# Routing of a two-layer transformer's second attention moved from a stage of its own into the attention's steps

## The reference

```python
def _L1_attn_ref(x, Wkqv, bkqv, Wp, bp):             # 16 heads, keys and queries of 128, values of 8
    ...
    A = jnp.einsum('bhnd,bhmd->bhnm', q, k) / jnp.sqrt(jnp.float32(Dm))
    A = jax.nn.softmax(jnp.where(mask[None, None], A, -jnp.inf), axis=-1)    # causal
    sa = jnp.einsum('bhnm,bhmd->bnhd', A, v).reshape(Bm, Nm, Dm)
    return sa @ Wp + bp

x = _layernorm(x + _L1_attn_ref(x, ...))             # called x3 below

def _moe_forward(x, centroid, Wg, bg, W1, b1, W2, b2):       # 8 experts, 2 per token
    d2 = sum(xs * xs) + sum(centroid * centroid) - 2.0 * (xs @ centroid.T)
    dist = jnp.sqrt(jnp.maximum(d2, 1e-12))
    w, sel = jax.lax.top_k(dist, K)                  # the two farthest centroids
    w = softmax(w)
    out = sum over the chosen e of w_e * ((silu(xs @ Wg[e] + bg[e]) * (xs @ W1[e] + b1[e])) @ W2[e] + b2[e])
```

## Time and profile before

| | us |
|---|---|
| median of three runs (2514.0, 2520.67, 2524.66) | 2520.67 |
| the profiled execution's own time | 2512.72 |
| its span | 2511.0 |
| `layer0`, 0 to 599.5 | 599.5 |
| `attention1`, 599.5 to 1863.1 | 1263.6 |
| `route1`, 1863.1 to 2126.8 | 263.7 |
| `experts1`, 2126.8 to 2433 | 306.2 |
| `combine1`, 2433 to 2511 | 78 |

### The profile page before, as it was taken

One profiled execution on the slowest core, in us unless ns is written; L12 is line 12 of the kernel. 1 busy time (PEld: TensorE's weight loads), 2 busy tenths in 40 slices (PEclk: granted clock), 3 DMA queues, 4 the chain that ended last, 5 costly groups with the idle time before them and its releaser, 6 DMA issues. The chain is left out here.

```text
span 2511.0 us, 67688 instructions
## 1 busy us (share of the span) xinstructions
PE 2272.6 (91%) x16828; PEld 1709.2 (68%) x16829; DVE 1888.3 (75%) x6162; ACT 1605.6 (64%) x4162; POOL 1015.9 (40%) x1979
## 2 busy tenths in 40 slices
PE   5999999997999999999999999999989991999960
PEld 3777777774666666666666666666657771999960
DVE  6888888871888888888888888888864552666658
ACT  2555555553777777777777777777753331667664
POOL 5676676671222222222222222222213666555542
PEclk9999999997999999999999999999985555999985
DMA  1011001001000000000000000000021111222225
GB/s 33 28 31 33 30 29 33 27 26 47 1 0 0 0 0 0 0 0 0 0 0 0 0 0 0 0 0 0 0 70 61 58 62 52 57 60 60 61 69 168
DMA packets 77583, 68.83 MB, mean 27 GB/s; under 512 B 10573, under 2 KB 70490, under 8 KB 77036
## 3 DMA queue, kind: packets, MB, share of 16 engines
q1 hardware_dynamic: 68830, 50.88, 6.9%
q0 software_dynamic: 8704, 17.39, 2.1%
HBM read 33.55 MB, written 22.62 MB: 22 GB/s over the span
## 5 line engine op out<-in xcount | busy, mean ns | idle before, releaser
L1017 DVE SCALAR_TENSOR_TENSOR restT<-ps_t,leadT 128x512 f16<-128x512 f32 (+1 forms) x768 | 462.8, 603 | 147.3 <-ACT leadT L978 95.3
L892 PE MATMUL ps_s<-xT_all,qm 128*128 (+1 forms) x1024 | 492.8, 563 | 11.8 <-issue 10.9
L978 ACT ACTIVATE leadT<-ps_t 128x512 f16<-128x512 f32 (+1 forms) x768 | 400.4, 522 | 151.0 <-PE ps_t L908 151.0
L908 PEld LDWEIGHTS ps_t<-ident,p 128*128 128x128 f32 x2560 | 320.8, 141 | 216.4 <-issue 180.9
L908 PE MATMUL ps_t<-ident,p 128*128 128x128 f32 x2560 | 405.4, 273 | 1.2 <-DVE restT L1017 0.5
L846 POOL CAST v_parts<-v_all 128x36 bf16 (+1 forms) x256 | 56.3, 220 | 805.8 <-PE ps_o L921 805.8
L1008 DVE CUSTOM_DVE_ANT_0 ps_s<-ps_s,mask 128x512 f32<-128x512 f32 (+1 forms) x512 | 320.1, 625 | 46.7 <-PE ps_s L892 46.6
L970 ACT ACTIVATE p<-ps_s,neg_max 128x512 f32<-128x512 f32 (+1 forms) x512 | 323.5, 632 | 4.6 <-DVE neg_max L1008 4.1
L892 PEld LDWEIGHTS ps_low<-xT_all,qm 128*128 128x128 f32 x1024 | 195.1, 191 | 135.8 <-issue 122.5
L884 PE MATMUL ps_qm<-xT_all,m_head 128*128 (+1 forms) x512 | 275.2, 619 | 0.3 <-issue 0.3
L267 POOL TENSOR_TENSOR pv_prod<-probs,kv 128x2048 f32<-128x2048 f32 x64 | 259.6, 4080 | 0.1
(11 more groups left out here) (222 smaller groups left out, 4570.2 us busy)
## 6 DMA issues: line engine op xcount, KB each, us to landing
row_in<-rows_dram SPq DMA_DIRECT2D x136, 64.5 KB, 1.9
y<-results SPq DMA_DIRECT2D x32, 256.0 KB, 3.3
xT<-in_xT SPq DMA_DIRECT2D x32, 128.0 KB, 2.2
xres<-in_xT SPq DMA_DIRECT2D x32, 128.0 KB, 2.1
x_all<-x SPq DMA_DIRECT2D x32, 128.0 KB, 2.0
xT_all<-x2T SPq DMA_DIRECT2D x32, 128.0 KB, 2.0
x_all<-x SPq DMA_DIRECT2D x16, 256.0 KB, 2.3
out_x<-x SPq DMA_DIRECT2D x16, 256.0 KB, 2.2
```

Of the source, the lines that this page charges most:

```text
L892: mm = pe.matmul(ps_s[n], qm[j][:, n * P:(n + 1) * P], xT_all[:, bass.ds(sequence(u) * S, (n + 1) * P)], start=True, stop=True)
L908: mm = pe.transpose(ps_t[g][:, at + n * P:at + (n + 1) * P], probs[i][:, n * P:(n + 1) * P], ident[:, :])
L978: act.activation(leadT[j][g][:, :], ps_t[g][:, 0:width[g]], ACT.Copy, scale=RAISE)\
L1017: dve.scalar_tensor_tensor(out=restT[j][g][:, :], in0=ps_t[g][:, 0:width[g]], scalar=RAISE, in1=leadT[j][g][:, :], op0=ALU.mult, op1=ALU.s ...
```

## The change

`route1` is gone. A sequence's routing is done within the attention's steps of the next sequence: in step h of sequence b, each engine calls `route(b - 1, h)` behind its `step`. Only the last sequence's routing comes after the attention. One PSUM bank (`ps_r`, P × 512) that was spare serves it in turn for the transposes, for two halves of products, and for the count.

```diff
+                for b in range(2):
+                    for h in range(H):
+                        one(b, h)
+                        if b:
+                            route(b - 1, h)
+                with eng.Fori(2, NG - 1) as b:
+                    for h in range(H):
+                        step(b, h, True, True, True, True)
+                        route(b - 1, h)
+                for h in range(H):
+                    one(NG - 1, h)
+                    route(NG - 2, h)
```

```diff
+                def bias_x2T(g):
+                    pool.wait_ge(c_ready, 5)
+                    when(pool, proj_ps, 2 * g)
+                    pool.tensor_tensor(x2T[:, :], xT_all[:, bass.ds(g * S, S)], bias[:, :].to_broadcast([P, S]), ALU.add)\
+                        .then_inc(x2T_sb, 1)
...
+                def scatter(g, places):
+                    pool.wait_ge(slots_ready, g + 1)
+                    wait_alone(pool, rows_ready, 3 * (g + 1), pool_passed)
+                    for n in places:
+                        r, i = n // B, n % B
+                        pool.indirect_dma_start(
+                            out=rows_dram[:, :], out_offset=bass.IndirectOffsetOnAxis(ap=slot_idx[:, n:n + 1], axis=0),
+                            in_=blk(rows[r], i, ROW), in_offset=None).then_inc(scattered, 16)
...
+                def project(g, a):
+                    pe.wait_ge(saT_sb, g + 1)
+                    pe.wait_ge(x2T_sb, g + 1)
+                    if a:
+                        pe.wait_ge(normed, B * g + 2)
+                    for i in range(2):
+                        pe.matmul(blk(ps_r, i, WD), blk(x2T, 2 * a + i), id_c[:, :], start=True, stop=False)
+                        mm = pe.matmul(blk(ps_r, i, WD), blk(saT, 2 * a + i), wp_c[:, :], start=False, stop=True)
+                    mm.then_inc(proj_ps, 1)
```

More of the change, by code:

```diff
@@ L719, in layer0, with skewed, one, earlier @@
     nc.all_engine_barrier()
[L722 to L734, removed]
+def skewed(eng, n, begin, ahead, depth, stride, step):
+    def one(s):
+        step(s // stride, s % stride, lambda p: 0 <= s - p < n)
+    whole = (n - ahead - begin) // stride * stride
+    for s in range(begin):
+        one(s)
+    first, j0 = begin // stride, begin % stride
+    with eng.Fori(first, first + whole // stride) as u:
+        for j in range(j0, j0 + stride):
+            step(u + j // stride, j % stride, lambda p: True)
+    for s in range(begin + whole, n + depth):
+        one(s)
+def earlier(u, j, p, stride=2):
+    return u + (j - p) // stride, (j - p) % stride
+ROW = P + 1
+NOWHERE = 1 << 22
+def attention1(nc, sh, wqT, wkT, bq, wp, wpT, bp, bv1, cT, keep, routing, expert_loads):
+    xT_all, v_all, x_all, ident = keep
+    rows_dram, squares_all, tile_expert, tile_row = routing
+    S, B, NG = sh.seq, sh.blocks, sh.batches
+    NT, LIST, TILES = sh.tiles, sh.list_rows, sh.listed_tiles
+    NK = NG * H
+    WD = P + E
     PV = DH + 1
@@ new lines, in step, with route @@
+                def step(b, h, nxt, last, this, older):
+                    if nxt:
+                        load_head(*before(b, h, -1))
+                        split_values(*before(b, h, -1))
+                def route(g, h):
+                    if h == 2:
+                        bias_x2T(g)
+                    if h == 4:
+                        inverse(g, 0)
+                    if h == 7:
+                        inverse(g, 1)
+                    if h == 10:
+                        make_rows(g)
+                        keep_tops(g)
+                    if h == 13:
+                        scatter(g, range(0, 3))
+                    if h == 14:
+                        scatter(g, range(3, 6))
+                    if h == 15:
+                        scatter(g, range(6, 8))
@@ L860, in _ @@
                 load_head(0, 0)
                 split_values(0, 0)
-                steps(step)(pool)
+                steps(step, route)(pool)
+                pool.wait_ge(pads_ready, 2)
+                for e in range(E):
+                    pool.indirect_dma_start(
+                        out=rows_dram[:, :], out_offset=bass.IndirectOffsetOnAxis(ap=pad_idx[:, e:e + 1], axis=0),
+                        in_=filler[:, :], in_offset=None).then_inc(pads_scattered, 16)
+                pool.wait_ge(scattered, 16 * 2 * B * NG)
@@ L925, in weighted_values, with step @@
                     mm.then_inc(out_ready_ps, 1)
-                def step(u, j, nxt, last, this, older):
-                    b = before(u, j, 1)
+                def step(b, h, nxt, last, this, older):
+                    last_step = before(b, h, 1)
                     if this:
-                        scores(u, j, 3)
+                        scores(b, h, 3)
+                    if this and h == 2 and not (isinstance(b, int) and b == 0):
+                        turn_sa(b - 1)
                     if last:
-                        turn(*b, 1)
+                        turn(*last_step, 1)
@@ L944, in _, with route @@
+                def route(g, h):
+                    if h == 2 and isinstance(g, int) and g == NG - 1:
+                        turn_sa(g)
+                    if h == 3:
+                        project(g, 0)
+                    if h == 6:
+                        project(g, 1)
+                    if h == 11:
+                        count(g)
                 queries(0, 0)
-                steps(step)(pe)
+                steps(step, route)(pe)
             @block.scalar
```

863 lines of the change are left out of this document (394 added, 469 removed).

## The result

The changed kernel takes 2639.09 us (median of four runs, 2637.32 to 2646.6) where the kernel before takes 2517.93 us: 1.0484 times as long, interval 1.0451 to 1.0517. It is slower, as forecast, and by less: the forecast was 2705 us with a range of 2575 to 2785. The profiled execution has 2637.6 us.

What follows compares the result with a forecast made beforehand. PE was taken to bound the attention, with POOL 0.15 us ahead. From 2512.7 us: −263.7 routing, +46 last sequence, −20 loop, +50 and +2 PE, +238 POOL, +35 DVE and ACT, +105 clock gave 2705 us, range 2575 to 2785.

Steps and rivals of the forecast that it cites:

- last sequence: Behind the attention: the last sequence's routing stays uncovered, including a 21 us chain before its first scatter; +46 us.
- POOL's small groups: POOL's routing at steps h 2, 4, 7, 10 delays PE's queries by 1.05, 2.15, 2.15 and 1.25 us.
- POOL's scatters: POOL's scatters at steps h 13, 14, 15 delay PE's queries by 3.5, 3.5 and 2.25 us per sequence.
- clock: PE's granted clock falls after the three longest stalls, at the scatters: 7 us per sequence, +105 us, bounds 0 and 11.
- PE, DVE and ACT: Routing's work within the attention: PE 3.3 us, DVE and ACT 2.3 us per sequence, +50 and +35 us.
- POOL's term: Routing on POOL ahead of the head's matrix copy stalls PE 15.9 us per sequence: +238 us, bounds +177 and +282.
- the signs that were to show the forecast right: In the attention: seven POOL waits per sixteen steps, 16 us per sequence; 1620 to 1700 us; clock below 0.95.
- The wait for the pick: At step h 11 PE's count waits for DVE's pick: 1.1 us per sequence.
- The loop's term: Attention loop from four to sixteen steps: 49 fewer turns at 0.41 us each, −20 us.
- rival 3: The sixteen-step loop is fetched anew: 2.3 us a turn, unless POOL's scatters cover it, 30 us, 2735 us in all; 8%.
- Rival 1: PE's clock holds through the attention's stalls, all else as forecast: 2600 us; 22%.
- Rival 2: POOL's routing is hidden, needing about 3.5 us of copy lead; no stall or clock fall: 2362 us; 10%.

Runs made afterwards that it cites:

- e1: The change with POOL's copy of the head's matrix issued one step earlier, ahead of the routing's work: 0.9511 of the kernel before, 2413.18 us.
- e8: The kernel before with only POOL's copy of the head's matrix issued one step earlier, as a control: 1.0006 of the kernel before.
- e9: The change with unused filler products on PE in the stalls at the scatters, POOL's order kept: 1.0272 of the kernel before.
- e6: The change with early copy, bias_x2T at h 8, scatters spread thinner, count moved to h 12 and places to h 13: 0.9354 of the kernel before.
- e3: The change with the early copy and scatters 2, 2, 2, 2 over h 13, 14, 15 and the next h 0: 0.9425 of the kernel before.
- e2: The change with only the scatters respread as 2, 2, 2, 2 over h 13, 14, 15 and the next h 0: 1.0394 of the kernel before.
- e10: The change with the 13 turns of its loop written out: 1.0366 of the kernel before.

## Why the prediction was nearly right

The mechanism was the right one, and e1 and e8 prove it from both sides. Against its terms (per sequence where they count fifteen times):

| term | forecast | measured |
|---|---|---|
| routing stage | −263.7 | −263.7 |
| last sequence | +46 | +43.5 |
| POOL's small groups | 6.6 each sequence | 6.5 |
| POOL's scatters | 9.25 | 11.2 to 11.7 (e9) |
| clock | 7 | 3.7 to 3.2 (change less e9) |
| PE, DVE and ACT | 5.6 | 4.4 |
| turns and small gaps of before | −1.3 | −2.2 |
| sum per sequence | 27.2 | 23.6 |

The last sequence's chain took 19.4 us from the attention's end to its first scatter, forecast 21. The small groups came out at 1.17, 2.10, 2.07 and 1.14 us for 1.05, 2.15, 2.15 and 1.25.

Two sizes were off, in opposite directions. **The clock** was counted at 2.0 us after both long stalls and 3.0 after the third. The step that failed took every one of the three stalls to drop it and to cost the whole 2 to 3 us, on the strength of one place. In the trace after, the third interval (interval 0 of the next sequence) kept 1.00 in five of the twelve sequences (895.78 to 903.34 us, with 5.49 us of PE's time), and the falls at the first two stalls cost 1.6 and 1.3 us net. 3.3 to 3.8 us too much make −50 to −57 us over fifteen sequences. **The scatters** were 1.9 to 2.4 us short, +29 to +37 us: 0.6 us pass between the split and the first of them, and it takes 1.09 us and not 0.96. The sum of both was 16.25 us in the forecast and is 14.9; that the two errors cancel in part is luck.

PE, DVE and ACT cost 1.2 us less than forecast, −18 us. A part of it is the 0.5 us for PE's switches, which stand in no row: the transposes and the eight products lengthen intervals 2, 4 and 7 by 0.44, 0.81 and 0.93 us, 2.2 in all, for 2.3 without switches. The small gaps of before that went with the turns are −13. That leaves some 15 of the missed 67 us to the ends: the first routed sequence has no scatters in front of it and took 95.5 us. The bounds of POOL's term, 11.8 and 18.8 us, do not come out of its groups as listed, which give 14.0 and 17.6; the measured 17.7 to 18.2 (6.5 with the scatters) lie at the upper end. Of the signs that were to show the forecast right, the attention's time is just outside (1606.7 us for 1620 to 1700), the clock at its edge (0.95 for below 0.95), and PE's wait for the matrix was 13.9 us per sequence for 16.

The wait for the pick was about right: 1.24 us of interval 12 go with it in e6, for 1.1. The loop's term was wrong in its reason: the step that kept 0.41 us per turn took the fetch of a body of four steps for that of sixteen. The long turn costs 2.2 us, as rival 3 had it (2.3), but two scatters stand behind it on POOL and hid nearly all of it in the change, which that rival had named as its condition.

Rival 1, a clock that holds (2600 us), is what e9 made: the change's 2639 us less 43 are 2596 us. Rival 2, POOL hidden (2362 us, 0.94 of before), is what e3 made by hand: 0.9425. Its condition, a lead of 3.5 us, was missing in the change's order.

## What to carry to other kernels

Work that is put into another engine's idle time belongs behind what the bottleneck asks of that engine next, not ahead of it: here the same instructions cost 1.0484 in one place and 0.9511 in the other. Idle share says nothing of that; the distance from the engine's result to its use does, and here it was 0.1 us on an engine three quarters idle. When a loop's body grows, measure its turn anew, and look whether the instruction queues begin to bring packets at each turn.

## What had not been expected of the hardware

- Behind an indirect DMA, POOL's next split, which has a wait, begins 0.8 to 1.0 us after the row's end (e1, e3), and the first DMA of a group begins 0.4 to 0.6 us after its predecessor. A copy of the matrix whose wait had long been met follows at once (2090.76 in the change).
- The length of a standstill of PE alone did not decide whether the granted clock fell. 1.8 us at `inverse` left it at 1.00 each time; 2.0 to 2.4 us in interval 0 of the change, behind two longer ones, came with a lower clock in seven of twelve sequences; 2.6 to 2.8 us did so in some (e2); 3.9 us in every sequence of the change (interval 14 at 0.72 to 0.84), but 3.7 us in e10 left it at 1.00 twice (1467.09 to 1475.85 and 1863.15 to 1871.91 us). Products that nobody needs kept it up.
- A loop of sixteen attention steps costs 2.2 us at each turn; the same code without a loop costs nothing in fetching, with 1.70 MB for PE's queue.
